# The small statistics products of a fused norm and convolution, as 64-row halves, with the statistics a quarter image earlier

## What is computed

```python
m, s = mean(x), var(x)            # per image and channel, over 128x128
z = (x - m) / sqrt(s + 1e-5)
avg = z.mean(axis=(2, 3))         # 32 numbers for an image
wk = sigmoid(avg @ w1.T + b1)     # 32 x 3 x 3 taps for an image
y = depthwise_conv3x3(z, wk) + conv_bias
out = x + (z - y) * fscale * z + y
```

## Time and profile before

| what | value |
|---|---|
| median of 3 runs | 348.79 us (347.7 to 349.02) |
| profiled execution, its own time | 347.56 us |
| its span | 345.8 us |
| granted TensorE clock, mean | 0.998 |
| busy: PE, PEld, DVE, ACT, POOL | 313.9, 249.8, 252.7, 198.2, 244.2 us |
| DMA | 77.47 MB, mean 224 GB/s |

### The profile page before, as it was taken

One profiled execution on the slowest core, in us unless ns is written; L12 is line 12 of the kernel. 1 busy time (PEld: TensorE's weight loads), 2 busy tenths in 40 slices (PEclk: granted clock), 3 DMA queues, 4 the chain that ended last, 5 costly groups with the idle time before them and its releaser, 6 DMA issues.

```text
span 345.8 us, 6194 instructions
## 1 busy us (share of the span) xinstructions
PE 313.9 (91%) x2176; PEld 249.8 (72%) x2176; DVE 252.7 (73%) x598; ACT 198.2 (57%) x322; POOL 244.2 (71%) x337
## 2 busy tenths in 40 slices
PE   0149999999999999999999999999999999999994
PEld 0127877877777787777878777777778777778883
DVE  3975787868778786877878686877878687554635
ACT  1246565837656573855756484675658376565910
POOL 1434686886968587795958779596868859687663
PEclk9999999999999999999999999999999999999999
DMA  7997037648293855828294683829376322133355
GB/s 292 417 423 322 3 137 289 267 154 367 104 348 140 320 237 189 368 105 333 121 359 198 220 337 128 351 101 380 154 277 280 136 104 104 70 136 138 136 207 205
DMA packets 10364, 77.47 MB, mean 224 GB/s; under 512 B 1275, under 2 KB 1374, under 8 KB 2654
## 3 DMA queue, kind: packets, MB, share of 16 engines
q1 hardware_dynamic: 10334, 77.08, 56.8%
HBM read 39.33 MB, written 37.75 MB: 223 GB/s over the span
## 4 chain that ended last, share of the span: by engine, by line
PE 63%; DVE 16%; POOL 14%; issue 2%; DMA 2%; ACT 1%; SPq 0%; POOLq 0%; ACTq 0%
PE conv_ps L377 18%; PE conv_ps L374 17%; PE conv_ps L370 12%; POOL outs L677 11%; PE conv_ps L366 7%; DVE outs L465 4%; DVE pieces L423 3%; PE dyn_ps L345 3%; DVE row_stats L433 3%; DMA xs<-x 2%; DVE dyn L442 2%; PE stat_ps L334 2%; PE stat_ps L339 2%; PE stat_ps L329 2%; DVE own_dyn L438 2%
## 5 line engine op out<-in xcount | busy, mean ns | idle before, releaser
L677 POOL TENSOR_TENSOR outs<-outs,linear 128x1152 f32<-128x1152 f32 x63 | 165.9, 2633 | 50.6 <-DVE outs L465 50.6
L374 PE MATMUL conv_ps<-xs,taps 64*128 64x320 f32 (+1 forms) x512 | 180.9, 433 | 0.0
L370 PE MATMUL conv_ps<-xs,taps 64*128 64x320 f32 (+1 forms) x512 | 172.9, 417 | 0.0
L366 PE MATMUL conv_ps<-xs,taps 64*128 64x320 f32 (+1 forms) x512 | 165.8, 403 | 0.0
L377 PE MATMUL conv_ps<-xs,taps 64*128 64x320 f32 (+1 forms) x512 | 165.2, 402 | 0.0
L465 DVE SCALAR_TENSOR_TENSOR outs<-xs,beta,conv_ps 128x576 f32<-128x576 f32 x128 | 103.3, 807 | 80.9 <-PE conv_ps L377 80.9
L565 ACT ACTIVATE linear<-xs,offset,gain 128x576 f32<-128x576 f32 x128 | 108.9, 856 | 1.4 <-POOL outs L677 1.4
L423 DVE BATCH_NORM_STATS2 pieces<-xs 128x6 f32<-128x64 f32 (+1 forms) x256 | 101.3, 448 | 5.7 <-DMA xs<-x 5.7
L370 PEld LDWEIGHTS conv_ps<-xs,taps 64*128 64x128 f32 x512 | 91.4, 187 | 15.4 <-issue 6.2
L377 PEld LDWEIGHTS conv_ps<-xs,taps 64*128 64x128 f32 x512 | 95.4, 186 | 8.7
L543 ACT ACTIVATE xs<-xs,neg_mean 128x576 f32<-128x576 f32 x128 | 97.4, 764 | 0.0
(11 more groups left out here) (48 smaller groups left out, 129.2 us busy)
## 6 DMA issues: line engine op xcount, KB each, us to landing
xs<-x SPq DMA_DIRECT2D x30, 1188.0 KB, 10.2
out<-outs SPq DMA_DIRECT2D x30, 1152.0 KB, 4.8
xs<-x SPq DMA_DIRECT2D x4, 594.0 KB, 6.1
out<-outs SPq DMA_DIRECT2D x3, 576.0 KB, 2.8
out<-outs SPq DMA_DIRECT2D x2, 288.0 KB, 2.6
cst<-const SPq DMA_DIRECT2D x1, 271.5 KB, 7.9
w1s<-w1r SPq DMA_DIRECT2D x1, 111.4 KB
gates<-gate SPq DMA_DIRECT2D x1, 8.0 KB
```

What stands on the lines that cost most here:

```text
L366: nc.tensor.matmul(bank_of(i, g, h), pair(i, g, 0, 0), columns(i, g, h, 0, 1), start=False, stop=False).then_inc(even_done, 1)
L370: nc.tensor.matmul(bank_of(i, g, h), pair(i, g, 0, 2), columns(i, g, h, 0, 0), start=True, stop=False)
L374: nc.tensor.matmul(bank_of(i, g, h), pair(i, g, 1, 1), columns(i, g, h, 1, 0), start=False, stop=False)
L677: nc.gpsimd.tensor_tensor(tile, tile, linear[:, PAIR * k:PAIR * (k + 1)].rearrange("p g n -> p (g n)"), ALU.add).then_inc(out_ready, 1)
```

## The change

The four small products are each written as products over 64 partitions. `mean`, `spread_stats` and `dynamics` become an even half that starts an accumulation and an odd half that adds to it, one bank step later and after a wait for the even half's completion. `averages` only needs partitions 0 to 63 and becomes one such product. In image i they stand before banks 0 (`averages`), 2 and 3 (`dynamics`), 7 and 8 (`mean`), 11 and 12 (`spread_stats`); those that serve images 1 and 2 keep later places. VectorE's `bn` runs six groups further ahead than image i+2, in place of four; `rows` of image i+2 stands right behind `product(i, 2)`, and `own_taps` ahead of it. The scaling of the counts moves from VectorE to ScalarE (`count`). On ScalarE and GpSimd the steps of the statistics move forward to match.

```diff
-EARLY = 4
+
+START_AHEAD, AHEAD = 4, 6
...
-    counts = np.ones((PARTS, GROUPS, 6), np.float32)
-    counts[row < ROWS - STEP] = 0.0
-    put("counts", counts)
+    put("counts", (row >= ROWS - STEP).astype(np.float32))
...
+            def mean_even(j):
                 pe.wait_ge(rows_done, j + 1)
-                nc.tensor.matmul(mean_ps, const_of("average"), row_stats[:, j % 2, :, 0],
-                                 start=True, stop=True).then_inc(mean_done, 1)
-
-            def spread_stats(j):
+                nc.tensor.matmul(mean_ps, const_of("average")[0:HALF], row_stats[0:HALF, j % 2, :, 0],
+                                 start=True, stop=False).then_inc(mean_half, 1)
+
+            def mean_odd(j):
+                pe.wait_ge(mean_half, j + 1)
+                nc.tensor.matmul(mean_ps, const_of("average")[HALF:], row_stats[HALF:, j % 2, :, 0],
+                                 start=False, stop=True).then_inc(mean_done, 1)
+
+            def spread_even(j):
                 pe.wait_ge(moments_ready, j + 1)
-                nc.tensor.matmul(zstats_ps, const_of("average"), moments[:].rearrange("p a g -> p (a g)"),
-                                 start=True, stop=True).then_inc(zstats_done, 1)
+                nc.tensor.matmul(zstats_ps, const_of("average")[0:HALF], moments[0:HALF].rearrange("p a g -> p (a g)"),
+                                 start=True, stop=False).then_inc(zstats_half, 1)
+
+            def spread_odd(j):
+                pe.wait_ge(zstats_half, j + 1)
+                nc.tensor.matmul(zstats_ps, const_of("average")[HALF:], moments[HALF:].rearrange("p a g -> p (a g)"),
+                                 start=False, stop=True).then_inc(zstats_done, 1)
+
 
             def averages(j):
                 pe.wait_ge(avg_cols_ready, j + 1)
-                nc.tensor.matmul(avg_ps, avg_cols[:], const_of("phase"), start=True, stop=True).then_inc(avg_rows_done, 1)
-
-            def dynamics(j):
-                pe.wait_ge(constants_set, 2)
+                nc.tensor.matmul(avg_ps, avg_cols[0:HALF], const_of("phase")[0:HALF],
+                                 start=True, stop=True).then_inc(avg_rows_done, 1)
+
+            def dynamics_first(j):
+                pe.wait_ge(constants_set, 1)
                 at_least(pe, matrices_ready, 2 * j)
                 pe.wait_ge(avg_rows_ready, j + 1)
-                nc.tensor.matmul(dyn_ps[:, 0:GROUPS * SETS * SLOTS], avg_rows[:], w1s[:],
-                                 start=True, stop=True).then_inc(dyn_done, 1)
+                nc.tensor.matmul(dyn_ps[:, 0:GROUPS * SETS * SLOTS], avg_rows[0:HALF], w1s[0:HALF],
+                                 start=True, stop=False).then_inc(dyn_half, 1)
+
+            def dynamics_second(j):
+                pe.wait_ge(dyn_half, j + 1)
+                nc.tensor.matmul(dyn_ps[:, 0:GROUPS * SETS * SLOTS], avg_rows[HALF:], w1s[HALF:],
+                                 start=False, stop=True).then_inc(dyn_done, 1)
...
             def chain(i, at):
-                if i + 1 < B:
-                    if at == 3:
-                        averages(i + 1)
-                    if at == 5:
-                        dynamics(i + 1)
-                if i + 2 < B:
-                    if at == 10:
-                        mean(i + 2)
-                    if at == 13:
-                        spread_stats(i + 2)
-
-            mean(0)
-            spread_stats(0)
+                j = i + 1
+                late = j < 3
+                if j < B:
+                    if at == (3 if late else 0):
+                        averages(j)
+                    if at == (5 if late else 2):
+                        dynamics_first(j)
+                    if at == (6 if late else 3):
+                        dynamics_second(j)
+                j = i + 2
+                late = j < 3
+                if j < B:
+                    if at == (10 if late else 7):
+                        mean_even(j)
+                    if at == (11 if late else 8):
+                        mean_odd(j)
+                    if at == (14 if late else 11):
+                        spread_even(j)
+                    if at == (15 if late else 12):
+                        spread_odd(j)
...
             def rows(j):
                 dve.wait_ge(pieces_done, GROUPS * (j + 1))
-                nc.vector.tensor_tensor(pieces[:, j % 2, :, 1], pieces[:, j % 2, :, 1],
-                                        counts_ps.rearrange("p (g e) -> p g e", g=GROUPS),
-                                        ALU.mult).then_inc(counted_ready, 1)
                 dve.wait_ge(counted_ready, j + 1)
                 for g in range(GROUPS):
...
-            def ahead(i, first, last):
-                for g in range(first, last):
-                    j, g = (i + 2, g + EARLY) if g + EARLY < GROUPS else (i + 3, g + EARLY - GROUPS)
-                    if j < B:
-                        bn(j, g)
-                    if j < B and g == GROUPS - 1:
-                        rows(j)
...
+                if i == 0:
+                    for g in range(START_AHEAD):
+                        bn(2, START_AHEAD + g)
+                        product(0, g)
+                    own_taps(1)
+                    rows(2)
+                    bn(3, 0)
+                    product(0, 4)
+                    bn(3, 1)
+                    product(0, 5)
+                    bn(3, 2)
+                    matrices(1)
+                    product(0, 6)
+                    bn(3, 3)
+                    product(0, 7)
+                    for g in range(4, AHEAD):
+                        bn(3, g)
+                else:
+                    bn_ahead(i + 2, AHEAD, AHEAD + 1)
+                    product(i, 0)
+                    bn_ahead(i + 2, AHEAD + 1, GROUPS)
+                    product(i, 1)
+                    if nxt and i > 1:
+                        own_taps(i + 1)
+                    bn_ahead(i + 3, 0, 1)
+                    product(i, 2)
+                    if stats:
+                        rows(i + 2)
+                    bn_ahead(i + 3, 1, 2)
+                    product(i, 3)
+                    if nxt and i == 1:
+                        own_taps(i + 1)
+                    bn_ahead(i + 3, 2, 3)
+                    product(i, 4)
+                    if nxt and i > 1:
+                        matrices(i + 1)
+                    bn_ahead(i + 3, 3, 4)
+                    product(i, 5)
+                    bn_ahead(i + 3, 4, 5)
+                    if nxt and i == 1:
+                        matrices(i + 1)
+                    product(i, 6)
+                    bn_ahead(i + 3, 5, AHEAD)
+                    if i == B - 1:
+                        add_last(GROUPS - 2)
+                    product(i, 7)
...
+            def count(j):
+                act.wait_ge(consts_loaded, 16)
+                act.wait_ge(pieces_done, GROUPS * (j + 1))
+                nc.scalar.activation(pieces[:, j % 2, :, 1], pieces[:, j % 2, :, 1], ACT.Identity,
+                                     scale=const_of("counts")).then_inc(counted_ready, 1)
...
+                    if nxt and g == (2 if i < 2 else 0):
+                        copy_averages(i + 1)
+                    if nxt and g == (4 if i < 2 else 3):
+                        sigmoid(i + 1)
+                    if stats and g == (4 if i == 0 else 1):
+                        count(i + 2)
+                    if stats and g == (6 if i == 0 else 5):
+                        negative_mean(i + 2)
                     linear_part(i, g)
                     if nxt:
                         centre(i + 1, g)
-                    if nxt and g == 1:
-                        copy_averages(i + 1)
-                    if nxt and g == 3:
-                        sigmoid(i + 1)
-                    if stats and g == 4:
-                        negative_mean(i + 2)
-                    if stats and g == 6:
+                    if stats and g == (7 if i == 0 else 6):
                         copy_stats(i + 2)
...
                 add_pair(i, 0)
-                if nxt:
+                if nxt and i > 1:
                     scaled_taps(i + 1)
+                if stats and i > 0:
+                    second_moments(i + 2)
                 add_pair(i, 1)
-                if stats:
+                if nxt and i < 2:
+                    scaled_taps(i + 1)
+                if stats and i == 0:
                     second_moments(i + 2)
+                if stats and i > 0:
+                    deviation(i + 2)
+                    average_columns(i + 2)
                 add_pair(i, 2)
-                if stats:
+                if stats and i == 0:
                     deviation(i + 2)
                     average_columns(i + 2)
```

(72 more changed lines are left out.)

2 lines of the change are left out of this document (removed).

## The result

The changed kernel takes 366.15 us (median of 4 runs, two near 364.5 and two near 367.8) against 348.73 us: a ratio of 1.0506, 95% interval 1.0436 to 1.0575. The forecast was 345.4 with a range up to 356.5. The profiled execution took 364.53 us with a span of 362.7.

What follows compares the result with a forecast made beforehand. TensorE's own order was taken as the bound. Gains of 5.6, 1.1 and 0.1 us against losses of 0.5 (image 0) and 3.0 (start) gave -3.3: 344.2 profiled, 345.4 against the median, range 338.5 to 356.5.

Steps and rivals of the forecast that it cites:

- rival (e): Wait of some 2.5 us per image lowers the granted clock; first banks lose about 1 us, 13 times: 358; chance 0.05.
- The halves: Small products as halves cost 0.30, 0.48 and 0.21 us, odd ones nothing; 2.01 us saved per image.
- Rival (a): Halves keep program order, so each odd half also holds the even stream: 0.90 us an image, 358.0 in all; chance 0.15.
- (d): A half empties the array as the full product did, so the 2.01 saved is missing: above 370 us; chance 0.03.
- The wait before `mean`: TensorE waits before bank 7 for VectorE's product 2 and `rows`: 2.90 us in place of 1.36, a loss of 1.54.
- The start: Ahead of the first bank nothing hides the halves, so it comes 3.0 us later.
- image 0: Waits before bank 10 (3.1 us) and at `matrices` (0.7); the image loses 0.5 us.
- image 1: `mean` loses 1.17 us and `matrices` brings a wait of 0.7; the image gains 0.1.
- `count`: Moved to ScalarE; about 0.6 us with `sigmoid` in image 0's wait for `rows`, nothing in steady images.
- Rival (b): `averages` comes late through ScalarE and GpSimd, delaying bank 0 by 0.5 us an image, 12 times: 351.4; chance 0.17.
- images 2 to 13: Halves save 2.01 us and the wait before `mean` costs 1.54: 0.47 gained each, 5.6 us for twelve.
- image 14: Has neither `mean` nor `spread_stats`, and gains 1.1 us.

Runs made afterwards that it cites:

- Experiment 1: Changed kernel with five idle products of 256 columns, in the even half, ahead of `mean_even` in each image: 348.36 us, ratio 1.000 to the kernel before.
- experiment 6: Kernel before the change with one edit, full `mean` before bank 8 in place of bank 10: 389.41 us, ratio 1.1196.
- experiment 8: Experiment 7 with `negative_mean` two groups earlier, `copy_stats` one earlier, `averages` and both `dynamics` halves one bank later: 317.42 us, ratio 0.9127.
- Experiment 10: Experiment 9 with `rows` of image 2 ahead of product 3, `count` of image 2 one group earlier and of image 3 one later: 307.01 us, 0.883.
- experiment 9: Experiment 8 with the small products ahead of the first bank full again, except `averages` of image 0: 315.39 us, ratio 0.904.
- experiment 7: Changed kernel with `rows` of image i+2 ahead of product 2 and `own_taps` behind it: 362.72 us, ratio 1.0433.
- experiment 4: Kernel before the change with its four small products as halves, everything else, including the order, as before: 334.52 us, ratio 0.9605.
- experiment 3: Changed kernel with both `mean` halves one bank later (8 and 9) and nothing else: 338.89 us, ratio 0.9714.
- experiment 2: Changed kernel with two idle products, in place of five, ahead of `mean_even`: 349.03 us, ratio 1.0036.

## Why the prediction was wrong

**The failed step is the clock.** The sum put the fall of the clock behind the long wait at nothing, and rival (e), which is what happened, had a chance of 0.05 and a price of 1 us an image. Its mechanism was named rightly, its size was 1.68 us, nine times in eleven steady images, 15.1 us in all. The reason given for the small chance was that the clock is 1.00 where pauses are 1.25 us. But the pause that the same text had worked out was twice as long, and no row of before covered that. Of the 1.25 us, besides, TensorE as a whole was idle for 0.25 only the earlier trace rows, against 1.89 in the changed kernel. The unknown should have had a large chance and the range an upper end beyond the 358 that the text itself had for (e). Experiment 1 shows that these 15.1 us are the clock's, and experiment 6 that the wait alone brings it.

**The halves were right.** They cost 0.22, 0.48 and 0 for `averages`, `dynamics_first` and `dynamics_second`, against 0.30, 0.48 and 0. `spread_even` costs less than the 0.21 counted; the even stream around it, just before bank 11:

```profile
219.17 0.43 PE L386 MATMUL conv_ps<-xs,taps 64*128 64x320 f32 x1
...
219.44 0.29 PE L342 MATMUL stat_ps<-moments,cst 64*128 64x16 f32 x2
219.58 0.46 PE L390 MATMUL conv_ps<-xs,taps 64*128 64x256 f32 x1
```

The last pass before it makes the next due at 219.44, and that one began at 219.58, 0.14 later. Rival (a), each odd half in both streams, is out: the even stream has no gap at `dynamics_second` (207.29, above), and an image of experiment 8 leaves 0.06 us for all odd halves together. So is (d).

**The wait before `mean` was right.** 2.90 us were counted, 2.60 measured to the resumption, with 209.75 to 212.07 = 2.32 from product 1 to product 2 against a counted 2.31. A steady image without the fall takes 19.17, counted 19.41. With the wait filled (experiment 1), the kernel takes 348.36 where 345.4 was forecast.

**The start and image 0 were right, image 1 was not.** The first bank begins at 28.77 in place of 25.58, 3.2 us later; 3.0 was counted. Image 0 takes 22.72 us in place of 22.18, a loss of 0.54 where 0.5 was counted, and its two waits came too: bank 10 begins 2.95 us late (3.1 counted, with 0.11 for a slow first bank) and bank 0 of image 1 0.82 (0.7 counted). Image 1 was counted 0.1 faster than before and takes 9.0 us more, 28.88 in place of 19.90. For `count` the text had a term in image 0 only; elsewhere it cost nothing, by a look at the steady images. In image 1 it does cost:

```profile
57.44 0.34 ACT L623 ACTIVATE pieces<-pieces,cst 128x48 f32<-128x48 f32 x1 [5.59 <-DVE pieces L459]
...
59.10 0.25 ACT L604 ACTIVATE avg_rows<-stat_ps 99x128 f32<-99x128 f32 x1
```

```profile
59.50 0.48 PE L360 MATMUL dyn_ps<-w1s,avg_rows 64*128 64x288 f32 x1 [2.45 <-ACT avg_rows L604]
```

`count` waits 5.59 us for VectorE's `bn`, `copy_averages` is queued behind it, and TensorE stands 2.45 us at `dynamics_first`. A further 1.62 us went at `spread_even` of the same image. The clock fell here too and stayed down for about 10 us, three times as long as behind a wait of the steady images:

```profile
61.00:71.00 10.00, 8.47 (x38) 7.18 (x37) 3.31 (x14) 1.21 (x2) 0.30 (x1) 0.50 0.60 246
```

Experiment 10 moves `count` of image 3 behind `copy_averages` and `rows` of image 2 ahead of its product, and gains 8.4 us over experiment 9. Between the two profiled executions, TensorE's idle times in images 0 and 1 fall from 4.8 to 1.1 us, 3.7 of the 8.2 us; the rest goes with a mean clock of 0.998 in place of 0.986. That division is an estimate.

**Rival (b)** didn't come: no idle time of 0.15 us or more stands before `averages` in the steady images. The same chain through ScalarE and GpSimd did become the bound once the wait for `rows` was gone, at `spread_even` (experiment 7).

**The accounts.** 364.53 - 344.2 = 20.3 us are to be explained in the profiled execution. Nine falls are 15.1, and image 1 is 9.1. The other way, images 2 to 13 without the falls are 3.4 better than counted and image 14 is 0.6; the start is 0.2 worse, the end 0.2 better. That makes 20.2. Of the 9.1 in image 1, the waits of 2.45 and 1.62 us are 4.1; the remaining 5.0 agree with a clock of 0.82 over 28.88 us, 5.2, but no experiment separated the two.

## What to carry to other kernels

A small product over as many partitions as its neighbours, 64 here, cost a busy TensorE 0.13 to 0.48 us, and the same product over 128 partitions 0.91 to 1.36. But when the order is changed for it, look at what stands directly ahead of each waiting product. Where a wait depends on the product just issued, count the whole way through the other engine. A change that is a gain by itself (experiment 4, 13.6 us) can be lost in an order that comes with it. And price each wait of TensorE twice, once for its length and once for the clock behind it; a few idle products in it tell the two apart.

## What the runs showed of the hardware

- TensorE's clock fell to 0.50 behind idle times of 1.67 us (experiment 7, 8 of 11 steady images), 1.89 us (changed kernel, 9 of 11) and 2.19 us (experiment 6, 9 of 13). With 0.81 us (experiment 3) no steady image has a fall. With 1.34 us (experiment 2) none has one in the profiled execution, the fastest of ten; half of the runs have a lower mean clock.
- In the steady images a fall lasted 3.4 us and cost 1.44 us (experiment 6), 1.46 (experiment 7) or 1.68 (changed kernel). In images 0 and 1 falls of 6.8 us (experiment 9) and 10 us (changed kernel) are seen.
- The same wait sometimes escapes in each of the kernels with waits of 1.67 us or more, and so does the 2.02 us in image 0 of the changed kernel; what decides it stays open.
- Idle products in one half of the array were enough to keep the clock up for both (experiment 1).
- A full product between halves cost 0.91 to 1.36 us, a waiting time of 0.20 to 0.25 in two of them included; the even halves of the same products cost 0.13 to 0.48, and the odd ones together at most 0.06 in an image (experiment 8).
